# A decoder layer on one core: first products of the gated network made inside the preparation, its loop over batches written out, and steps of the first phase reordered

## What is computed

```python
x = layernorm(x + linear_attention(x))   # 16 heads, chunks of 64 tokens, gate, output projection
x = layernorm(x + expert(x, fside, ctx)) # per batch: two int8 "smooth quant" linears with silu(gate)*up between
x = layernorm(x + moe_ffn(x))            # 8 low-rank experts, top 2 by token, on a shared gated network

# inside moe_ffn, for the two experts chosen by each token:
h1 = x @ w1.T + 2 * (x @ A1.T @ B1.T)    # base1: same for all experts
h3 = x @ w3.T + 2 * (x @ A3.T @ B3.T)
out += weight * (silu(h1) * h3) @ (w2.T, A2, B2)
```

## Time and profile before

| | |
|---|---|
| time, median of 3 runs | 1122.92 us (1122.57 to 1123.58) |
| time of the profiled execution | 1123.99 us |
| its span | 1122.0 us |
| busy: PE, PEld, DVE, ACT, POOL | 92%, 72%, 64%, 36%, 26% |
| first phase, second phase | to 405 us, from 405 us |

### The profile page before, as it was taken

The page is one execution under the profiler, slowest core; times in us unless marked ns, Lnnn a source line. Parts: engine busy times, 40 slices in busy tenths (PEclk is TensorE's granted clock), DMA queues, the critical chain, the costliest instruction groups (busy, mean ns, idle before and its releaser), DMA issues.

```text
span 1122.0 us, 13753 instructions
## 1 busy us (share of the span) xinstructions
PE 1032.4 (92%) x4911; PEld 812.3 (72%) x4920; DVE 720.4 (64%) x1150; ACT 402.6 (36%) x623; POOL 295.3 (26%) x245
## 2 busy tenths in 40 slices
PE   3799999989999868999999899989999999999996
PEld 2677777767777636778777777767777867888885
DVE  4565786785676657868647858565976773654442
ACT  4234333334332233434342344444253533322231
POOL 2347674543224400201322200042100131200021
PEclk9899999999999968999999999999999999999999
DMA  7116664130021044434381244445153327134421
GB/s 265 59 65 238 212 237 147 52 104 10 10 87 38 1 145 161 143 120 164 108 304 40 94 157 150 162 148 206 38 180 135 113 98 258 57 141 155 173 66 56
DMA packets 47861, 142.98 MB, mean 127 GB/s; under 512 B 3496, under 2 KB 14632, under 8 KB 42160
## 3 DMA queue, kind: packets, MB, share of 16 engines
q1 hardware_dynamic: 28720, 118.71, 29.2%
q10 hardware_dynamic: 19072, 23.35, 6.6%
HBM read 114.66 MB, written 27.39 MB: 127 GB/s over the span
## 4 chain that ended last, share of the span: by engine, by line
PE 42%; DVE 14%; issue 3%; ACT 2%; DMA 2%; DVEq 0%; ACTq 0%
PE f_h L106 7%; PE f_h L107 7%; PE f_h L108 7%; PE f_h L2196 4%; PE f_y L106 2%; PE f_y L108 2%; PE f_y L107 2%; DMA f_down_raw<-in_down_stream 2%; DVE f_work L1937 2%; DVE f_q_mem L1957 2%; DVE f_work L1929 2%; PE f_y L2386 1%; PE f_z_sum L106 1%; DVE f_row_max L2007 1%; PE f_z_sum L107 1%
## 5 line engine op out<-in xcount | busy, mean ns | idle before, releaser
L106 PE MATMUL f_h<-f_xT_hi,f_up 128*128 128x512 f32 x352 | 140.6, 399 | 1.0 <-issue 1.0
L107 PE MATMUL f_h<-f_xT_hi,f_up 128*128 128x512 f32 x352 | 138.6, 394 | 0.0
L108 PE MATMUL f_h<-f_xT_lo,f_up 128*128 128x512 f32 x352 | 137.8, 391 | 0.0
L106 PE MATMUL ring<-w_hi,xT_hi 128*128 128x512 f32 x256 | 109.4, 427 | 24.8 <-POOL xT_lo L428 22.3
L1516 POOL TENSOR_TENSOR f_down_lo<-f_down_raw,f_down_hi 128x512 fp32r<-128x512 f32 x44 | 61.0, 1389 | 229.7 <-ACT f_down_hi L1566 229.7
L1723 ACT ACTIVATE f_work<-f_h 128x512 f32<-128x512 f32 x88 | 52.4, 596 | 172.9 <-PE f_h L2196 116.6
L1929 DVE TENSOR_TENSOR f_work<-f_work,f_weightT 128x512 f32<-128x512 f32 x88 | 65.6, 746 | 73.8 <-ACT f_work L1723 73.7
L1527 POOL TENSOR_TENSOR weights<-weights,f_rows 128x512 f32<-128x512 f32 (+1 forms) x24 | 31.2, 1331 | 294.6 <-ACT f_rows L1648 186.0
L1937 DVE TENSOR_TENSOR f_work<-f_h,f_work 128x512 f32<-128x512 f32 x88 | 60.9, 692 | 71.6 <-PE f_h L108 65.5
L108 PE MATMUL ring<-w_lo,xT_hi 128*128 128x512 f32 x256 | 102.7, 401 | 0.0
L107 PE MATMUL ring<-w_hi,xT_lo 128*128 128x512 f32 x256 | 102.3, 400 | 0.0
(11 more groups left out here) (315 smaller groups left out, 2280.0 us busy)
## 6 DMA issues: line engine op xcount, KB each, us to landing
f_up<-up_scratch SPq DMA_DIRECT2D x44, 1408.0 KB, 6.2
f_down_raw<-in_down_stream ACTq DMA_DIRECT2D x44, 256.0 KB, 3.5
x_tok<-x_scratch SPq DMA_DIRECT2D x7, 1024.0 KB, 9.3
scaled_w<-in_up_stream SPq DMA_DIRECT2D x6, 704.0 KB, 5.3
up_scratch<-q_mem SPq DMA_DIRECT2D x6, 704.0 KB, 3.7
up_scratch<-scaled_w SPq DMA_DIRECT2D x6, 704.0 KB, 3.1
x_tok<-in_x SPq DMA_DIRECT2D x4, 1024.0 KB, 5.5
out<-x_tok SPq DMA_DIRECT2D x8, 512.0 KB, 3.2
```

The lines of the kernel that those rows point to most:

```text
L106: pe.matmul(out, lhs_hi, rhs_hi, start=start, stop=False)
L107: pe.matmul(out, lhs_lo, rhs_hi, start=False, stop=False)
L108: return pe.matmul(out, lhs_hi, rhs_lo, start=False, stop=stop)
```

## The change

1. First phase, POOL, tile 8: all four pieces of `scale_weights` come behind tile 9's `rotate`.
2. First phase, ACT: `x_hi(0)` moves to the head of the list, ahead of weight_hi(0) and weight_hi(1).
3. First phase, ACT, ends of batches: `qT_out(g + 1)` comes ahead of `deviation`.
4. First phase, DVE: row_scale(0, 0) goes behind `mask_state(8, 1)`; round_rows(0, 0) and clamp(0, 0) go to the head of tile 9; row_scale(0, 1) behind mask_state(9, 1); round_rows(0, 1) and clamp(0, 1) to the head of tile 10.
5. Second phase, batch 0's preparation: where a small product used h1 or h3 it uses the second layer's banks y0 and y1.
6. `first` is cut in two, `from_tokens` (the 12 matmuls and their waits) and `from_adapters` (the 3); for b = 0, f = 0 both `from_tokens` stand in the preparation, behind adapters_in(U3) and ahead of `masks_transposed`.
7. The loop over batches 0 and 1 is written out on every engine.

```diff
# POOL, tile loop
-                if g == 8:
-                    scale_weights(0, (0, 1))
                 if has_next(g):
                     rotate(g + 1, 0)
                     rotate(g + 1, 1)
                 if g == 8:
-                    scale_weights(0, (2, 3))
+                    scale_weights(0, range(TT))
# ACT
+            x_hi(0)
             weight_hi(0)
             weight_hi(1)
-            x_hi(0)
             x_hi(1)
...
+                if more:
+                    qT_out(g + 1)
                 if ends_batch(g) and more:
                     deviation(batch_of(g))
-                if more:
-                    qT_out(g + 1)
# DVE, ahead of mask_state(g, 1)
-                if g == 8:
-                    row_scale(0, 0)
                 if g == 9:
-                    row_scale(0, 1)
+                    round_rows(0, 0)
+                    clamp(0, 0)
+                if g == 10:
+                    round_rows(0, 1)
+                    clamp(0, 1)
# DVE, behind mask_state(g, 1)
                 if g == 8:
-                    round_rows(0, 0)
+                    row_scale(0, 0)
                 if g == 9:
-                    round_rows(0, 1)
+                    row_scale(0, 1)
# DVE, behind attT_lo(g)
-                if g == 8:
-                    clamp(0, 0)
-                if g == 9:
-                    clamp(0, 1)
# second phase
-        bank = h_ps + z_ps
+        def bank(b, k):
+            return (h_ps + z_ps)[k] if b or k > 1 else y_ps[k]
...
             prepare(0)
-            with eng.Fori(0, B - 2) as b:
-                hidden(b, True)
-                between(b, True, True)
-            hidden(B - 2, True)
-            between(B - 2, True, False)
-            hidden(B - 1, False)
-            between(B - 1, False, False)
+            for b in range(B):
+                hidden(b, b < B - 1)
+                between(b, b < B - 1, b < B - 2)
...
             def first(b, f, i):
-
+                if (b, f) != (0, 0):
+                    from_tokens(b, f, i)
+                from_adapters(b, f, i)
+
+            def from_tokens(b, f, i):
                 if i == 0:
                     pe.wait_ge(up_loaded[f % SLOTS], ...)
...
+
+            def from_adapters(b, f, i):
                 cols = slice(2 * D + i * P, 2 * D + (i + 1) * P)
...
                 adapters_in(b, U3)
+                from_tokens(b, 0, 0)
+                from_tokens(b, 0, 1)
                 masks_transposed(b)
```

More of the change, by code:

```diff
@@ L1575, in x_hi @@
                 sc.wait_ge(filled[k], PRIMED + n + 1)
-                sc.activation(xT_hi[:, c, :], bank[k][:, :], ACT.Copy).then_inc(xT_hi_ready, 1)
+                sc.activation(xT_hi[:, c, :], bank(b, k)[:, :], ACT.Copy).then_inc(xT_hi_ready, 1)
             def logits_out(b):
@@ L1580, in logits_out @@
                 sc.wait_ge(filled[k], PRIMED + n + 1)
-                sc.activation(logitsT[:, :], bank[k][0:E, :], ACT.Copy).then_inc(drained[k], 1)
+                sc.activation(logitsT[:, :], bank(b, k)[0:E, :], ACT.Copy).then_inc(drained[k], 1)
             def softmax_exp(b):
@@ L1597, in weights_out @@
                     sc.wait_ge(filled[k], PRIMED + n + 1)
-                    sc.activation(weightT[:, a, :], bank[k][:, :], ACT.Copy).then_inc(drained[k], 1)
+                    sc.activation(weightT[:, a, :], bank(b, k)[:, :], ACT.Copy).then_inc(drained[k], 1)
             def masked_hi(b, a):
@@ L1625, in load_weights @@
                     sc.wait_ge(q_ready, PRIMED + 6 * b + 4)
-                elif isinstance(b, int) and b == 0:
+                elif b == 0:
                     sc.wait_ge(consts_ready, PRIMED + 5)
@@ L1643, in channel_rows @@
                         sc.wait_ge(filled[k], PRIMED + n + 1)
-                        sc.activation(rows[:, i, 0:C], bank[k][:, 0:C], ACT.Copy).then_inc(drained[k], 1)
+                        sc.activation(rows[:, i, 0:C], bank(b, k)[:, 0:C], ACT.Copy).then_inc(drained[k], 1)
                     else:
@@ L1752, in hidden @@
                         quantised(b, 1, 1)
-                    if expert and f == 9 and not (isinstance(b, int) and b == B - 2):
+                    if expert and f == 9 and b != B - 2:
                         load_weights(b + 1, 0)
@@ L1966, in channel_ratio @@
                         k, n = slot(b, (MX0, MW0)[i])
-                        ready, free, done, source = filled[k], drained[k], freed(b, (MX0, MW0)[i]), bank[k]
+                        ready, free, done, source = filled[k], drained[k], freed(b, (MX0, MW0)[i]), bank(b, k)
                     else:
@@ L2202, in b_expert @@
             def b_expert(b):
-                return not (isinstance(b, int) and b == B - 1)
+                return b != B - 1
             def adapters_second(b, f):
@@ L2248, in x_transposed @@
                 if c == 0:
-                    if not (isinstance(b, int) and b == 0):
+                    if b:
                         pe.wait_ge(e_normed, PRIMED + TT * b)
                         pe.wait_ge(silu_ready, PRIMED + 2 * b * FT)
-                if c == 1 and not (isinstance(b, int) and b == 0):
+                if c == 1 and b:
                     pe.wait_ge(act_ready, PRIMED + 2 * b * FT)
@@ L2256, in x_transposed @@
                 for t in range(TT):
-                    last = pe.transpose(bank[k][:, bass.ts(t, P)], x2[:, t, bass.ts(c, P)], ident[:, :])
+                    last = pe.transpose(bank(b, k)[:, bass.ts(t, P)], x2[:, t, bass.ts(c, P)], ident[:, :])
                 last.then_inc(filled[k], 1)
@@ L2275, in logits_by_token @@
                 for t in range(TT):
-                    last = pe.matmul(bank[k][:, t * E:(t + 1) * E], logitsT[:, bass.ts(t, P)], ident[0:E, 0:E],
+                    last = pe.matmul(bank(b, k)[:, t * E:(t + 1) * E], logitsT[:, bass.ts(t, P)], ident[0:E, 0:E],
                                      start=True, stop=True)
@@ L2284, in adapters_in @@
                 for c in range(KT):
-                    last = matmul_split(pe, bank[k][:, :], a_hi[:, c, cols], a_lo[:, c, cols],
+                    last = matmul_split(pe, bank(b, k)[:, :], a_hi[:, c, cols], a_lo[:, c, cols],
                                         xT_hi[:, c, :], xT_lo[:, c, :], c == 0, c == KT - 1)
@@ L2305, in weights_spread @@
                     for t in range(TT):
-                        last = pe.matmul(bank[k][:, bass.ts(t, P)], weight[:, a, t:t + 1].to_broadcast([P, P]),
+                        last = pe.matmul(bank(b, k)[:, bass.ts(t, P)], weight[:, a, t:t + 1].to_broadcast([P, P]),
                                        ident[:, :],
@@ L2317, in first_maxima @@
                     for c in range(KT):
-                        last = pe.transpose(bank[k][:, bass.ts(c, P)], top[:, i, bass.ts(c, P)], ident[:, :])
+                        last = pe.transpose(bank(b, k)[:, bass.ts(c, P)], top[:, i, bass.ts(c, P)], ident[:, :])
                     last.then_inc(filled[k], 1)
```

14 lines of the change are left out of this document (7 added, 7 removed).

## The result

The changed kernel takes 1108.12 us (median of 4 runs, 1106.41 to 1109.25), the kernel before beside it 1122.74 us: a ratio of 0.9872, 95% interval 0.9855 to 0.9888. The profiled execution took 1108.33 us, with a span of 1106.5 us, 15.5 less than before. The forecast was 1107.8.

A forecast was written before the change was run, and what follows sets the result against it. PE is busy nearly throughout, so only its stops and lower clock were worth attacking. Gains 5.1 + 4.9 + 0.1 + 1.6 + 3.4 = 15.1 us took the median from 1122.92 to 1107.8; range 1103.5 to 1113.5.

The forecast's parts named there:

- start: First phase's start: with x_hi(0) first on ACT, POOL's split ends earlier and PE starts at 13.95, not 18.95; 5.1 us.
- tile 8: First phase: PE's wait for attended values goes and the tile takes 21.7 us instead of 26.60; 4.9 saved.
- ends of batches: First phase: q's transposed copy no longer waits for the variance, but the masked state still does; 0.1 us.
- preparation: Batch 0, second phase: 24 products moved ahead delay masks 1.8, yet PE is released 1.9 sooner; 1.6 us taken.
- loop: Way into batch 1: 5.07 us shorter without the jump back, 1.64 lost again in the tiles behind; 3.4 net.
- B: Rival at the start: a transfer ends last, and 4 of the 5.1 us go; 1111.8 us, chance 0.06.
- hold-up of DVE by the split: At the start, POOL's split blocks DVE's bias work beside it, so the first lower part comes 1.1 us later.
- the q product took 4.63 from there: At the start: from PE's first product to q's copy takes 4.63 us as before, so the copy comes at 18.5.
- A: Rival: tile 8's stop moves into tiles 9 and 10 and the 4.9 us go; 1112.7 us, chance 0.10.
- the four pieces stand in front of residual(8) and split(10): Tile 8 on POOL: the moved scale_weights pieces find room, as both steps behind them are needed only at the tile's end.
- Rival C: Preparation gives all its 7.3 us, as the silu's load slips in ahead; 1102.1 us, chance 0.05.
- Rival D: Written-out loop: instruction fetches stop engines 3.58 us each; with eight stops 1136.4 us, slower; chance 0.03.

The follow-up runs named there:

- f1: The changed kernel unaltered, timed again: 1107.99 us, against 1121.83 for the kernel before.
- e1: The kernel before with only x_hi(0) moved to the head of ACT's list: 1117.52 us, ratio 0.9963.
- e3: The kernel before with only the loop over batches written out: 1117.10 us, ratio 0.9951.
- g1: The kernel before with the loop kept on every engine but its jump back announced ahead: 1118.75 us, ratio 0.9974.
- e4: The changed kernel with small products in h1 and h3 again and tile f = 0's products in their old place: 1107.95 us, ratio 0.9885.
- f3: The changed kernel with only h1's twelve products ahead of the masks' transposes, h3's twelve behind the weights' spreading: 1108.00 us.
- f4: f3 plus DVE's bias work moved behind the first matrix's lower parts, against the changed kernel: 1107.76 us.

## Why the prediction came out right, by its steps

The time held, and so did the main mechanism of each term; one step failed, on POOL in tile 8, and some sizes were off. The terms stand like this (means over profiles with and without the edit; ends of batches: tile 4):

| step | forecast | runs |
|---|---|---|
| start | 5.1 | 4.6 |
| tile 8 | 4.9 | 3.5 (edit 4: 4.5; edit 1: -1.0) |
| ends of batches | 0.1 | 0.1 |
| preparation | 1.6 | 1.4 |
| loop | 3.4 | 4.2 |
| sum | 15.1 | 13.8 |

The medians differ by 14.6 in the first comparison and by 13.8 in the second (1121.83 to 1107.99). The part of the 15.5 of the one pair of profiles that no edit made is mostly tile 12's clock, 1.5. That the first median came within 0.3 of the forecast is partly luck: start and tile 8 gave 1.9 less than forecast, the loop 0.8 more, and the first comparison 0.8 more than the stages.

**Start.** The rival that a transfer ends last (B) is out: no wait for a DMA stands between the lower parts. The hold-up of DVE by the split was 1.10 of 1.1 forecast (13.29 against 12.19; 12.84 in f1, where the bias work began 0.35 sooner). What was mis-sized is "the q product took 4.63 from there", which is 5.84 in the first profile after. In f1 it is 4.86, and the third matrix's lower part comes at 19.68, where 19.65 was forecast. In the first profile after, all products of q are spaced 0.43 us, as products are elsewhere at a granted clock of 0.50 (before, 413.00 to 417.60); in f1 eight are, and before it was six; the others take 0.23. But the granted clock reads 1.00 in these stretches, so the rows don't tell what spaced them.

**Tile 8.** The wait for attended values went, and tiles 9 and 10 did not take it up (A is out: no stop of 1 us stands there). The step that failed is the one on POOL, "the four pieces stand in front of residual(8) and split(10); both are needed only at the tile's end". It asked who waits for POOL, and not which DVE instructions run beside it, although the forecast had priced just this hold-up at the start. That is the 1.0. With edit 4 alone tile 8 takes 21.81, where 21.7 was forecast. But that edit 4's whole gain, 4.5, comes near the 4.9 rests on two errors that nearly cancel. The 26.60 held a clock loss that e1, e3 and g1 don't have (24.97 to 25.05), so edit 4 saves 3.2 in tile 8 against them; and it saves 1.1 more in tiles 9 and 10 (47.00 against 48.10 to 48.18), where the forecast had no gain. Two readings were wrong, both on the safe side: rounding took 1.67 when alone and not 2.23 (in the earlier trace rows a step of POOL, 250.44 to 251.75, ran beside its start), and row_scale took 2.27 and not 1.4, so what replaces it in tile 9 exceeds it by 0.6 (1.67 + 1.23 - 2.27) and not by 2.0 (3.44 - 1.4).

**Ends of batches.** Tile 4: 22.33 before, 22.24 after. The three places together are not told apart from the clock.

**Preparation.** Each link came at its place; against U3's end the second part is released 1.84 earlier, 1.9 forecast (its terms add up to 442.26, not 442.35). Rival C is out: the load waited for `root`. The load's place behind `root` doesn't bear the forecast out, since e3 and e4 have it too; the release does. That 1.4 of it is left is partly luck. The forecast took off 0.3 for a fall of the clock behind PE's new stop; it reads 0.60 in the four microseconds from 431.88, and at tile f = 1's second part only 0.4 to 0.7 of the 1.84 is left. The rest comes back in that tile, where PE waits for DVE 1.44 us before and 0.79 after (not at all in f1), which was not forecast. The forecast had priced the delay of the masks, 1.8; f3 shows that it need not have been paid.

**Loop.** The shape of the term held: the way in is 5.2 shorter (5.07 forecast), and a part of that is lost again in the tiles behind it, where DVE paces PE. This part is 1.3, all in tile f = 1, and not 1.64; 4.0 is left up to tile f = 10 and 4.2 over the period. The windows of the one pair hide the loss (125.48 before, 125.92 after), since batch 1 of that one profile is short behind tile f = 10. Over the seven written-out kernels batches 1 and 2 are alike (periods of 177.56 and 177.60). Rival D has nothing for it: both ways in take 51.0, and behind batch 0's first tile no wait of PE in the written-out batches is longer than 2.5 us or without a name.

A kernel with edit 4 and f3's order but without edit 1 should be 1.0 + 1.8 below the changed one, as an estimate from the stages; it was not run, and f3 and f4, which were, are not measurably faster.

## What to carry to other kernels

When an elementwise step is moved on VectorE or GpSimd, list what the other runs in the new place: edit 1 looked free by its waiters and cost 1.0 us through its neighbours. Work that fills a stop belongs into the stop itself; what is put ahead of a step that others wait for is free only up to the time for which that step's result lay ready (2.24 us here). A loop of few passes can be tested for its jump alone: one engine's stop of 3.6 us and the clock behind it (1.6) were its price, less the 1.2 us that PE then waited for DVE in the next tile.

## What was not expected of the hardware

- The same stop of PE, 1.49 us in tile 12, was followed by a granted clock of 0.7 in one profile and 1.00 in another, and the tile took 1.5 us more. Terms of this size need several profiles.
- A stop's price can exceed its length: behind the 3.12 us for which PE waited on DVE at batch 1, 19 matmuls took 4.11 us at a clock of 0.58; behind a wait of 0.58 us the same stretch, 20 by the trace, took 2.51 at 1.00.
- An announced jump back cost DVE 0.63 us, an unannounced one 3.58 to 3.92.
